# One exponential over 2048 columns for a pair of heads where their PSUM windows are neighbours, in a transformer layer on eight cores

## What is computed

```python
def _L0_attn_ref(x, Wq, Wk, Wv, Wo, bo):
    q = (x @ Wq).reshape(b, l, n, d)
    k = (x @ Wk).reshape(b, l, n, d)
    v = (x @ Wv).reshape(b, l, n, d)
    attn = jnp.einsum('bind,bjnd->bnij', q * SCALE, k * SCALE)
    attn = jax.nn.softmax(attn.astype(jnp.float32), axis=-1)
    out = jnp.einsum('bnij,bjnd->bind', attn, v)
    return out.reshape(b, l, n * d) @ Wo + bo
def _L0_ffn_ref(x, ...):
    h = silu(tlin(x, w1_w, w1_s)) * tlin(x, w2_w, w2_s)
    h = gelu(tlin(h, h1_w, h1_s)); h = gelu(tlin(h, h2_w, h2_s))
    return tlin(h, w3_w, w3_s)
x = x + _layernorm(_L0_attn_ref(_layernorm(x), ...))
x = x + _layernorm(_L0_ffn_ref(x, ...))
```

## Time and profile before

| what | value |
|---|---|
| median of the runs shown | 10939.88 us (3 runs, 10360.82 to 10955.61) |
| the profiled execution's own time | 10145.56 us |
| its span, core 2, the slowest | 10144.0 us |
| spans of the eight cores | 10075.6 to 10144.0 us |
| mean granted TensorE clock of the cores | 0.896 to 0.899 |
| TensorE / ScalarE / VectorE / GpSimd busy | 80% / 29% / 18% / 11% |

### The profile page before, as it was taken

The page is one execution under the profiler, slowest core; times in us unless marked ns, Lnnn a source line. Parts: engine busy times, 40 slices in busy tenths (PEclk is TensorE's granted clock), DMA queues, the critical chain, the costliest instruction groups (busy, mean ns, idle before and its releaser), DMA issues.

```text
span 10144.0 us, 103608 instructions; the slowest of 8 cores (10075.6 to 10144.0 us)
## 1 busy us (share of the span) xinstructions
PE 8127.2 (80%) x37771; PEld 3475.0 (34%) x38276; DVE 1818.7 (18%) x2354; ACT 2964.7 (29%) x3426; POOL 1085.3 (11%) x1827
## 2 busy tenths in 40 slices
PE   3444558778787787786997998989979989899798
PEld 2222222212122222122444453444444534444444
DVE  3333322222322222222102011011020010110101
ACT  2222237557576575673001001010010010100000
POOL 5444430000000000000001001000010010000100
PEclk9676778888888888888999999999999999999999
DMA  7877860110101101102444334434434344344333
GB/s 240 208 199 213 214 177 1 38 29 9 38 1 38 38 1 38 27 12 75 150 150 141 150 145 145 151 142 148 150 133 154 144 145 154 141 149 150 133 150 139
DMA packets 249317, 1181.27 MB, mean 116 GB/s; under 512 B 33793, under 2 KB 33793, under 8 KB 177154
## 3 DMA queue, kind: packets, MB, share of 16 engines
q0 software_dynamic: 216576, 1048.76, 31.9%
q1 hardware_dynamic: 32258, 125.85, 3.8%
HBM read 1073.82 MB, written 134.22 MB: 119 GB/s over the span
## 4 chain that ended last, share of the span: by engine, by line
PE 46%; DMA 4%; issue 2%; DVE 1%; ACT 1%; DVEq 0%; SPq 0%; ACTq 0%; POOLq 0%
PE PQ L74 41%; PE PW L74 4%; DMA slab<-w2Ts 2%; DMA slab<-w1Ts 1%; DMA ybt<-y_s 1%; DMA slab<-h1Ts 0%; ACT HB L74 0%; DVE fs L74 0%; DVE ob L74 0%; DVE HB L74 0%; ACT L74 0%; PE ftr L74 0%; ACT fs L74 0%; DVE g_sb L74 0%; DVEq L71 0%
## 5 line engine op out<-in xcount | busy, mean ns | idle before, releaser
L74 PE MATMUL PQ<-HB,slab 128*128 128x512 bf16 x16056 | 3537.3, 380 | 64.1 <-DMA slab<-h1Ts 27.1
L74 PEld LDWEIGHTS PQ<-HB,slab 128*128 128x128 bf16 x16384 | 1605.9, 98 | 1995.5 <-issue 75.4
L74 ACT ACTIVATE ptring<-SS,cst 128x1024 bf16<-128x1024 f32 x2048 | 2071.5, 1215 | 671.2 <-PE SS L74 671.2
L74 ACT ACTIVATE HB<-PQ 128x1024 bf16<-128x1024 f32 x384 | 392.5, 1024 | 3577.6 <-PE PQ L74 3577.4
L74 PE MATMUL OP<-ptring,v_sb 128*66 128x512 bf16 x4096 | 1208.8, 411 | 87.8 <-DVE ocat L74 80.9
L74 PE MATMUL PQ<-g_sb,slab 128*128 128x512 bf16 x4008 | 947.7, 390 | 352.9 <-ACT HB L74 171.7
L74 PE MATMUL SS<-q_sb,k_sb 64*128 64x512 bf16 x4096 | 1070.6, 396 | 16.6 <-ACT ptring L74 9.0
L74 DVE RECIPROCAL rcp<-OP 1x512 bf16<-1x512 f32 x128 | 420.0, 3317 | 2028.7 <-PE OP L74 2028.7
L74 PE MATMUL ptr<-ident,pscb 128*128 128x128 bf16 x2816 | 315.9, 273 | 510.3 <-ACT pstg L74 270.6
L74 PEld LDWEIGHTS PQ<-g_sb,slab 128*128 128x128 bf16 x4096 | 395.1, 100 | 903.8 <-issue 493.2
L74 ACT COPY pstg<-ptr 128x512 bf16<-128x512 bf16 x704 | 381.8, 589 | 889.9 <-DMA h1Ts<-pstg 288.4
(11 more groups left out here) (87 smaller groups left out, 3048.7 us busy)
## 6 DMA issues: line engine op xcount, KB each, us to landing
slab<-h1Ts POOLq DMA_DIRECT2D x128, 2048.0 KB, 8.0
slab<-h2Ts POOLq DMA_DIRECT2D x128, 2048.0 KB, 8.1
natq<-h1w POOLq DMA_DIRECT2D x128, 512.0 KB, 5.8
natq<-h2w POOLq DMA_DIRECT2D x128, 512.0 KB, 5.6
slab<-w1Ts POOLq DMA_DIRECT2D x128, 512.0 KB, 4.1
slab<-w2Ts POOLq DMA_DIRECT2D x128, 512.0 KB, 4.0
slab<-w3Ts POOLq DMA_DIRECT2D x32, 2048.0 KB, 8.5
h1Ts<-pstg POOLq DMA_DIRECT2D x256, 128.0 KB, 6.0
```

The costliest lines, as they stand in the source:

```text
L74: ins = getattr(e, meth)(*args, **kw)
```

## The change

A new function `emit_exp2` takes the exponentials of both heads of a step with one ScalarE instruction of 2048 columns. It is used where the two windows that the step claimed are neighbours in `SS` (`wo == we + 1`, that is windows 0,1 or 1,2). Where they are windows 2 and 0, two instructions of 1024 columns stay. The slots of `ptring` are now picked by the parity of the step, 0 and 1 or 2 and 3, so that the two slots are neighbours too. The one instruction waits for the odd head's S (which comes after the even one's) and for the O matmuls that last read both slots. Both windows and both slots are handed on by its single semaphore increment. Nothing else is changed.

```diff
+                    def emit_exp2(hp, d, smm, we, ie, io, rse, rso):
...
+                        p.wait("scalar", TE, smm)
+                        for rs in (rse, rso):
+                            if rs in ring_owner:
+                                p.wait("scalar", TE, opair[ring_owner[rs]])
...
+                        ct = p.op("scalar", "activation",
+                                  ptring[:, rse * 1024:rse * 1024 + 2048],
+                                  SS[:, we * 1024:we * 1024 + 2048],
+                                  AF.Exp, scale=cst[:, 2:3], inc=True)
+                        ss_exp[Pe] = ss_exp[Po] = ct
...
+                        ring_rel[ie] = ring_rel[io] = (AE, ct)
...
-                    rs_ctr = [0]
-
-                    def next_rs():
-                        rs_ctr[0] = (rs_ctr[0] + 1) % 4
-                        return rs_ctr[0]
...
-                        emit_exp(2 * hp, d, se, we, ie, next_rs())
-                        emit_exp(2 * hp + 1, d, so, wo, io, next_rs())
+                        pr = (t % 2) * 2
+                        if wo == we + 1:
+                            emit_exp2(hp, d, so, we, ie, io, pr, pr + 1)
+                        else:
+                            emit_exp(2 * hp, d, se, we, ie, pr)
+                            emit_exp(2 * hp + 1, d, so, wo, io, pr + 1)
```

More of the change, by code:

```diff
@@ L554, in emit_exp @@
                         ring_rel[idx] = (AE, ss_exp[P])
+                    def emit_exp2(hp, d, smm, we, ie, io, rse, rso):
+                        Pe = (g * NH + 2 * hp) * NPR + d
+                        Po = (g * NH + 2 * hp + 1) * NPR + d
+                        p.wait("scalar", TE, smm)
+                        for rs in (rse, rso):
+                            if rs in ring_owner:
+                                p.wait("scalar", TE, opair[ring_owner[rs]])
+                        ring_owner[rse] = Pe
+                        ring_owner[rso] = Po
+                        ct = p.op("scalar", "activation",
[3 more added lines that the diff above has]
+                        ss_exp[Pe] = ss_exp[Po] = ct
+                        exp_ring[Pe] = rse
+                        exp_ring[Po] = rso
+                        ring_rel[ie] = ring_rel[io] = (AE, ct)
                     def emit_O(h_i, d):
```

## The result

The changed kernel takes 1.0415 times as long as the kernel before, with a 95% interval of 1.0395 to 1.0436. The runs compared lie at 10535 to 10547 us against 10118 to 10122, so it is some 420 us. The bare medians, 10770.12 and 10913.11 us, can't be compared (they would make the changed kernel the faster one), since each mixes in runs in which the cores of one die or of both had a lower granted clock, and for the same reason the trace of every kernel is read on a core that has the full one in the attention part. For the changed kernel that is core 2, whose span is 10520.0 us.

What follows compares the result with a forecast made beforehand. ScalarE's exponentials were taken to bound the attention part. A cycle 1.30 us longer gave 6.1 us a head pair, about 390 us over 64, carried to the 10939.88 us median: 11330 us, range 10463 to 11550.

Steps and rivals of the forecast that it cites:

- What bounds the part: Attention part, 1490 to 4700 us: ScalarE's exponentials set the pace, 2.017 us a step; TensorE has 0.45 us of slack.
- The price of 2048 columns: One merged exponential in the attention part was claimed to take 1.98 us, between 1.86 and 2.12.
- The cycle: Three attention steps, two merged and one separate: claimed to take 7.35 us instead of 6.05, with ScalarE idle 0.89 and 0.5.
- the 103 us of saved work: Pure ScalarE work saved by merging 688 steps at 0.15 us each, claimed to be already inside the predicted loss.
- The 14 steps of a head pair: Steps of each head pair claimed to run at ScalarE's pace: 6.1 us lost a pair, 388 us over 64 pairs.
- The hole: ScalarE's idle time at the reciprocals of each head pair, 8.30 us, claimed to stay unchanged.
- The sum: Whole kernel: 390 us added, 3.6% to 3.8% slower; 10536 us on the profiled execution, 11330 on the median.
- The saved starts: Rival in the attention steps: ScalarE stays without holes and 103 us come through, 10837 us on the median; chance 0.06.
- the chain: Attention steps: both merged exponentials lie in full on it, with 3.39 us of TensorE work and handovers formerly beside ScalarE.
- The clock: Rival in the attention part: holes lower TensorE's clock, about 1010 us in all, 11950, or in part 11500 to 11600; chance 0.07.
- The smaller loss: Rival in the attention steps: the cycle gives back half, +195 us, 11135, under 2%; chance 0.10.
- both couplings: Merged attention steps: the exponential starts only with both S in PSUM and hands both windows on only at its end.

Runs made afterwards that it cites:

- the coupled pair: Changed kernel with each merged exponential split into two of 1024 columns, still waiting for both S and releasing both windows at the second's end: ratio 1.0484 to the kernel before.

## Why the prediction was right

- *What bounds the part.* Right. ScalarE paces the steps of the kernel before: taking S matmuls away from TensorE leaves its exponentials at 3160.8 against 3162.1 us.
- *The price of 2048 columns.* 1.98 us was taken from 1.11 us and a slope of 0.85 ns a column out of the earlier trace rows; it is 1.967. The bounds of 1.86 and 2.12 were wider than needed. By the budget that the Trainium skill gives ("ScalarE: Activation LUTs", Rules for kernel authors), about 0.3 us for an ACTIVATE and 0.83 ns per element, it would be 2.00 us (an estimate), and the trace, with 1.967 us for an instruction that starts after a wait, agrees. What the prediction drew from it, that an instruction less saves 0.3 us, does not show: the coupled pair lasts 2.12 us and the merged one 1.97, so 0.15.
- *The cycle.* 7.35 us was worked out, 7.37 measured; the idle times of 0.89 and 0.5 us are 0.94 and 0.49. Small errors cancel in it: from the end of S to the exponential it is 0.21 to 0.24 us, not 0.15, and the four S matmuls side by side take 0.61 us, not 0.65. The prediction also says that the 103 us of saved work are inside. They are not. The exponentials of a cycle take 5.95 us (3.98 and 1.97) where three steps took 6.05, so 0.10 us a cycle, some 30 us in all, because two of the instructions now start after a wait.
- *The 14 steps of a head pair.* Too many, and the restart behind the hole was put at nothing. With 14 steps it is 1.32 x 14/3 x 64 = 394 us, and the exponentials take 433.6 longer. ScalarE's timeline on core 2 has 288 waits of 0.94 us and 271 of 0.49, so some 280 settled cycles and not 299, which is 370 us. The other 64 us, 1.0 a head pair, go mostly to the restarts: its other waits under 4 us add up to 86 us, where the kernel before has 26. I had let those steps stay as they are. In one restart the holes are 1.36, 0.78 and 0.31 us before the cycle settles, where the earlier trace rows has a single 0.31:

```profile
2875.81 1.97 ACT L74 ACTIVATE ptring<-SS,cst 128x2048 bf16<-128x2048 f32 x1 [1.36 <-PE SS L74]
2878.56 2.12 ACT L74 ACTIVATE ptring<-SS,cst 128x1024 bf16<-128x1024 f32 x2 [0.78 <-PE SS L74]
2880.98 1.97 ACT L74 ACTIVATE ptring<-SS,cst 128x2048 bf16<-128x2048 f32 x1 [0.31 <-PE SS L74]
```

- *The hole.* Predicted to stay at 8.30 us. It is now 7.57, 7.85, 8.51 or 8.86 us, 8.24 on average, so this holds in the mean. ScalarE's idle time that S ends rose by 464 us, not by some 490.
- *The sum.* 390 us (3.6% to 3.8%) against some 420 (4.15%). Carrying it to the median gave 11330 us, well above the median measured, 10770.12, and outside the forecast's own 11257 to 11412. The median was the wrong thing to carry it to: of the eight runs, four lie at 10535 to 10547 and four at 10993 to 11497, and 10770.12 is the mean of 10546.93 and 10993.32, a time that no run took. That it fell inside the wide range (10463 to 11550) says nothing on the mechanism. On the profiled execution's own time the sum gave 10536, and the runs compared lie at 10535 to 10547. That close a hit is luck: the loss is 30 us too small, and the starting point of 10145.56 us is 25 us above the 10118 to 10122 of the runs compared.
- *The rivals.* The saved starts did not win: the 0.15 us of a merged step after a wait is there and is buried in the chain. The clock did not fall (0.86). The smaller loss did not come. What I had not seen is that most of the loss needs both couplings: the prediction named both in one breath, and only the experiments told them apart. The late start alone costs nothing, the late release alone 209 us, and both together, without the wide instruction, 515.

## What to carry to other kernels

Before two instructions that share a ring buffer are merged, look whether the ring has a free place while the merged one runs. With three windows, one that holds two turned 0.15 us saved in a merged step into 0.44 us lost in every step of the cycle. Whether a fourth window would bring the saving out was not run. Ask of a merged instruction both when it can start and what it holds until it ends. Here either alone was free or cheap (0 and 0.16 us a step), and the two together closed the chain (0.54). And look at the periodic hole first: the one that the profile showed beside the steps, 8.30 us at each head pair, was worth 4% with a copy of the accumulators, where all the saved instruction starts together were put at 103 us, 1%.

## What the runs showed that I had not expected

A small matmul that claims a window of the ring costs more than its own time. With two claims the hole was 1.28 us or more in each head pair, with one 0.50. I had expected the windows to be held until VectorE had copied them, and the traces do not show that. In the rows above the first copy is done at 1540.71 us, and S starts at 1541.81, 0.98 us after O, as soon as TensorE comes to it. In the other holes over 1 us of this core it is the same. What costs is the order of TensorE's instructions: each claim waits for one more exponential (0.52 and 0.67 us), O and S stand behind it, and TensorE loses its lead over ScalarE.

The longer holes have one thing more, a lower clock. Behind the spreads before 1508.97 us, where the hole is 2.49 us, TensorE's granted clock is 0.56, and in the hole of 1.32 us it is 1.00 (after the stretch and its length, busy us and instructions by engine, then clock, DMA share, GB/s):

```profile
1506.03:1509.90 3.87, 3.87 (x13) 1.10 (x12) 2.01 (x3) 1.38 (x2) 0.00 (x0) 0.56 0.00 0
1538.30:1542.60 4.30, 3.11 (x15) 0.95 (x15) 2.26 (x4) 2.98 (x4) 0.00 (x0) 1.00 0.00 0
```

There the four S matmuls take 1.04 us and not 0.61. What TensorE did before was much the same in both, so why the clock fell in the one is open.
